# A transformer block on one core: projections moved ahead of a sum over values, gathered rows combined tile by tile, a table read one step sooner

## What is computed

```python
h = _layernorm(x) * (1 + ca) + sa
q = einsum('bpm,hmd->bphd', h, Q_w) + Q_b      # k and v likewise
logits = where(causal_mask, NEG, einsum('bqhd,bkhd->bhqk', q, k) / sqrt(128))
attn = einsum('bhqk,bkhd->bqhd', softmax(logits), v)
x = x + ga * (einsum('bqhd,hdm->bqm', attn, O_w) + O_b)
h = _layernorm(x) * (1 + cb) + sb
...
topk_scores, topk_idx = top_k(softmax(h @ Wr + router_bias), 4)
yb = einsum('ech,ehd->ecd', silu(xb @ Wg) * (xb @ Wu), Wd)     # xb: the tokens of each expert's slots
out[tok] += yb[eid, pos] * w                                    # 4 rows of yb per token
out = out + einsum('nsh,shd->nd', silu(h @ Sg) * (h @ Su), Sd)  # shared part
x = x + gb * out
```

## Time and profile before

| | us |
|---|---|
| median of 3 runs | 2115.46 |
| lowest and highest run | 2114.06, 2116.05 |
| the profiled execution, its time | 2119.06 |
| the profiled execution, its span | 2117.3 |

### The profile page before, as it was taken

The page is one execution under the profiler, slowest core; times in us unless marked ns, Lnnn a source line. Parts: engine busy times, 40 slices in busy tenths (PEclk is TensorE's granted clock), DMA queues, the critical chain, the costliest instruction groups (busy, mean ns, idle before and its releaser), DMA issues.

```text
span 2117.3 us, 33076 instructions
## 1 busy us (share of the span) xinstructions
PE 2014.0 (95%) x9863; PEld 1501.2 (71%) x9865; DVE 1381.3 (65%) x3219; ACT 1103.8 (52%) x1638; POOL 386.7 (18%) x409
## 2 busy tenths in 40 slices
PE   6899999999999999999999999999999989999997
PEld 4667667676676677676676776667877768777775
DVE  7677686686686686776866866846545833333375
ACT  3566575676575575665766755623333134444310
POOL 5211010010110110110100101633000132222364
PEclk8999999999999999999999999999999999999998
DMA  6488888888888878878888888994431098989664
GB/s 214 95 162 161 162 162 162 162 162 161 159 165 162 173 151 171 166 156 165 162 162 161 162 161 164 214 212 151 129 106 30 1 299 286 312 279 324 187 191 152
DMA packets 932173, 366.06 MB, mean 173 GB/s; under 512 B 754800, under 2 KB 885920, under 8 KB 932128
## 3 DMA queue, kind: packets, MB, share of 16 engines
q1 hardware_dynamic: 921888, 331.93, 69.5%
q0 software_dynamic: 10240, 33.56, 5.2%
HBM read 138.86 MB, written 41.94 MB: 85 GB/s over the span
## 4 chain that ended last, share of the span: by engine, by line
PE 65%; SPq 15%; DMA 8%; DVE 4%; issue 4%; POOL 3%; ACT 1%; DVEq 0%; POOLq 0%; ACTq 0%
SPq L473 14%; PE gen L1559 9%; PE gen L1561 9%; PE gen L1560 9%; PE strip L1559 7%; PE strip L1560 6%; PE strip L1561 6%; PE strip L1851 4%; PE pv L1559 4%; PE pv L1561 3%; PE pv L1560 3%; DMA wd_sb<-in_L_ffn_Wd 3%; DMA pT<-p_lo 2%; PE strip L1858 2%; DVE acc L1541 1%
## 5 line engine op out<-in xcount | busy, mean ns | idle before, releaser
L1171 DVE SCALAR_TENSOR_TENSOR p_lo<-exps,rinv,p_hi 128x512 f16<-128x512 f32 (+3 forms) x256 | 395.4, 1560 | 27.9 <-ACT p_hi L864 24.3
L855 ACT ACTIVATE exps<-exps,nbias 128x128 f32<-128x128 f32 (+15 forms) x256 | 306.3, 1197 | 136.7 <-DVE nbias L1157 136.7
L864 ACT ACTIVATE p_hi<-exps,rinv 128x512 f16<-128x512 f32 (+3 forms) x256 | 338.1, 1351 | 15.1 <-DVE rinv L1166 6.7
L1559 PE MATMUL strip<-kT_hi,qT_hi 128*128 128x512 f32 (+3 forms) x640 | 238.3, 372 | 14.4 <-DVEq L1248 6.3
L1147 DVE TENSOR_SCALAR_CACHE_REDUCE exps<-strip 128x512 f32<-128x512 f32 x384 | 249.1, 685 | 1.8 <-PE strip L1561 1.8
L1559 PE MATMUL pv<-pT,v 128*128 128x512 f16 (+3 forms) x640 | 223.3, 349 | 21.0 <-DMA pT<-p_lo 19.7
L1560 PE MATMUL strip<-kT_lo,qT_hi 128*128 128x512 f32 (+3 forms) x640 | 234.4, 366 | 0.0
L1561 PE MATMUL strip<-kT_hi,qT_lo 128*128 128x512 f32 (+3 forms) x640 | 234.1, 366 | 0.0
L710 POOL TENSOR_TENSOR wq_lo<-wq_raw,wq_hi 128x512 fp32r<-128x512 f32 x16 | 20.8, 1300 | 1105.2 <-ACT wq_hi L834 1105.2
L1560 PE MATMUL pv<-pT,v 128*128 128x512 f16 (+3 forms) x640 | 222.1, 347 | 0.0
L1561 PE MATMUL pv<-pT,v 128*128 128x512 f16 (+3 forms) x640 | 218.8, 347 | 0.0
(11 more groups left out here) (237 smaller groups left out, 4433.5 us busy)
## 6 DMA issues: line engine op xcount, KB each, us to landing
at_dram<-at_f SPq DMA_DIRECT2D x64, 256.0 KB, 2.6
wg_sb<-in_L_ffn_Wg SPq DMA_DIRECT2D x64, 256.0 KB
wu_sb<-in_L_ffn_Wu SPq DMA_DIRECT2D x64, 256.0 KB
wd_sb<-in_L_ffn_Wd SPq DMA_DIRECT2D x64, 256.0 KB
yb_dram<-yb SPq DMA_DIRECT2D x64, 256.0 KB
a_f<-at_dram SPq DMA_DIRECT2D x58, 256.0 KB, 2.9
pT<-p_hi SPq DMA_TRANSPOSE x320, 3.3
pT<-p_lo SPq DMA_TRANSPOSE x320, 3.3
```

The source lines that it names most:

```text
L855: nc.scalar.activation(row, row, ACT.Exp, bias=nbias[:, t:t + 1], accum_out=rsum[:, t:t + 1]).then_inc(row_probs, 1)
L864: nc.scalar.activation(p_hi16[:, 0:j + 1, t, :], row, ACT.Copy, scale=rinv[:, t:t + 1]).then_inc(p_hi, 1)
L1171: nc.vector.scalar_tensor_tensor(p_lo16[:, 0:j + 1, t, :], row, rinv[:, t:t + 1], p_hi16[:, 0:j + 1, t, :], ALU.mult, ALU.subtract).then_i ...
L1559: nc.tensor.matmul(o, a_hi, b_hi, start=start, stop=False)
```

## The change

Three edits. In stage 0 of every head, PE projects the next block's queries and keys ahead of the sum over values (values stay behind it); ACT and DVE take those two projections out before they make the probabilities of the block. In the last stage each of the 16 tiles is combined by itself, one or two per step from step 1 to 10, instead of in pairs with their operations interleaved. And the table of slots is read in step 10 instead of step 11.

The tables:

```diff
-        COMBINE = {step: pair for pair, step in enumerate((2, 3, 4, 6, 7, 8, 9, 10))}
+        COMBINE = {1: (0, 1), 2: (2, 3), 3: (4,), 4: (5, 6), 5: (7, 8), 6: (9,), 7: (10, 11), 8: (12, 13), 9: (14,),
+                   10: (15,)}
...
-                   11: [("table", 1)]}
+                   10: [("table", 1)]}
```

ACT, `stage`:

```diff
-                probs_hi(h, j, prev, 0)
-                probs_hi(h, j, prev, 1)
-                exp_row(h, j, 2)
-                exp_row(h, j, 3)
-                probs_hi(h, j, prev, 2)
-                probs_hi(h, j, prev, 3)
+                if j == 0:
+                    exp_row(h, j, 2)
+                    exp_row(h, j, 3)
+                    gen_hi_of("q", nxt[1], nxt[0])
+                    gen_hi_of("k", nxt[1], nxt[0])
+                    for t in range(TB):
+                        probs_hi(h, j, prev, t)
+                else:
...
                 if j == 0:
                     take_at_scale(h)
-                if nxt is not None:
+                    gen_hi_of("v", nxt[1], nxt[0])
+                elif nxt is not None:
                     for kind in "qkv":
                         gen_hi_of(kind, nxt[1], nxt[0])
```

DVE, `stage`:

```diff
+                if j == 0:
+                    row_inverse(h, j, 2)
+                    row_inverse(h, j, 3)
+                    gen_out_of("q", nxt[1], nxt[0])
+                    gen_out_of("k", nxt[1], nxt[0])
+                    probs_lo(h, j, 0)
+                    probs_lo(h, j, 1)
+                else:
...
```

DVE, `combine_beside`:

```diff
-                for k in range(TOPK):
-                    for t in pair:
-                        if k == 0:
-                            dve.wait_ge(g_landed[t % GATHS], (t // GATHS + 1) * 16 * TOPK)
-                        else:
-                            dve.wait_ge(dve_step, steps[0] - 1)
...
-                dve.sem_inc(combined, 2)
-                dve.sem_inc(gath_free, 2)
+                for t in COMBINE[step]:
+                    dve.wait_ge(g_landed[t % GATHS], (t // GATHS + 1) * 16 * TOPK)
+                    for k in range(TOPK):
+                        link(nc.vector.scalar_tensor_tensor(acc[:, t, :], gath[t % GATHS][:, k, :], w_top[:, t, k:k + 1],
+                                                            acc[:, t, :], ALU.mult, ALU.add))
+                    dve.sem_inc(combined, 1)
+                    dve.sem_inc(gath_free, 1)
```

PE, `stage`:

```diff
                 score(h, j)
+                if j == 0:
+                    project("q", *reversed(nxt))
+                    project("k", *reversed(nxt))
                 if prev is not None:
...
                     sum_values(hp, jp)
                 if nxt is not None:
                     hn, jn = nxt
-                    project("q", jn, hn)
-                    project("k", jn, hn)
+                    if j > 0:
+                        project("q", jn, hn)
+                        project("k", jn, hn)
```

More of the change, by code:

```diff
@@ L890, in stage @@
                 exp_row(h, j, 1)
-                probs_hi(h, j, prev, 0)
-                probs_hi(h, j, prev, 1)
-                exp_row(h, j, 2)
-                exp_row(h, j, 3)
-                probs_hi(h, j, prev, 2)
-                probs_hi(h, j, prev, 3)
+                if j == 0:
[6 more added lines that the diff above has]
+                else:
+                    probs_hi(h, j, prev, 0)
+                    probs_hi(h, j, prev, 1)
+                    exp_row(h, j, 2)
+                    exp_row(h, j, 3)
+                    probs_hi(h, j, prev, 2)
+                    probs_hi(h, j, prev, 3)
                 if prev is not None:
@@ L1180, in stage @@
                 score_row(h, j, 3)
-                probs_lo(h, j, 0)
-                row_inverse(h, j, 2)
-                probs_lo(h, j, 1)
-                row_inverse(h, j, 3)
+                if j == 0:
[6 more added lines that the diff above has]
+                else:
+                    probs_lo(h, j, 0)
+                    row_inverse(h, j, 2)
+                    probs_lo(h, j, 1)
+                    row_inverse(h, j, 3)
                 probs_lo(h, j, 2)
@@ L1188, in stage @@
                     hn, jn = nxt
-                    gen_out_of("q", jn, hn)
-                    gen_out_of("k", jn, hn)
+                    if j > 0:
+                        gen_out_of("q", jn, hn)
+                        gen_out_of("k", jn, hn)
                     if jn == 0:
@@ L1532, in combine_beside @@
                     return
-                pair = (2 * COMBINE[step], 2 * COMBINE[step] + 1)
                 dve.wait_ge(down_out, OUT_AFTER + step // (SC - AFTER0) * TB)
-                for k in range(TOPK):
-                    for t in pair:
-                        if k == 0:
-                            dve.wait_ge(g_landed[t % GATHS], (t // GATHS + 1) * 16 * TOPK)
-                        else:
-                            dve.wait_ge(dve_step, steps[0] - 1)
-                        ins = nc.vector.scalar_tensor_tensor(acc[:, t, :], gath[t % GATHS][:, k, :],
-                                                             w_top[:, t, k:k + 1], acc[:, t, :], ALU.mult, ALU.add)
-                        steps[0] += 1
-                        ins.then_inc(dve_step, 1)
-                dve.wait_ge(dve_step, steps[0])
-                dve.sem_inc(combined, 2)
-                dve.sem_inc(gath_free, 2)
+                for t in COMBINE[step]:
[5 more added lines that the diff above has]
+                    dve.sem_inc(gath_free, 1)
             for c in (6, 7):
```

## The result

The changed kernel took 2178.52 us (median of 4 runs, 2175.89 to 2180.56), the kernel before 2114.76 beside it (2113.86 to 2116.05): ratio 1.030, interval 1.0282 to 1.0318, so 3% slower. The forecast was 2180. The profiled execution took 2175.89 us with a span of 2174.1; the one of before had a span of 2117.3.

The account below looks back on a forecast made before the run. PE, busy 95% of the span, was taken as the bound. Heads +43.5, first head +6.3, clock +28, table -6.5 and combining -7 gave +64.3 us on 2119.06, 2183.4, stated as 2180 against the median; range 2146 to 2203.

Parts of the forecast that it names:

- The wait in each head: Later 15 heads: ACT waits for the values' transpose to land, PE ends 2.9 us later per head, +43.5 us.
- The first head: First head: probabilities made only after the keys' copy, so the values' transpose goes out later, +6.3 us.
- The clock: Behind PE's new idle stretch in 16 heads, matmuls run at half clock, 1.75 us each: +28 us, bounds 0 and 48.
- The rival in which the clock holds: Heads: everything as forecast but without the 28 us for the clock, 2152 us; chance 15%.
- Faster, with the values in time: Heads: the values' transpose lands in time, each head gains 1.9 us, 2073 us in all; chance 9%.
- The table: Start of the experts: slot table read a step earlier, PE's wait and the low clock behind it go, -6.5 us.
- The combining: Last stage: POOL's two waits go (5.1 us) and fewer operations follow the last gather (1.8 us), -7 us.
- The lower bound: Combining: +2 us if DVE, waiting in a step for a late tile, holds up PE's down product as often as now.
- The sum: Whole kernel: +43.5 + 6.3 + 28 - 6.5 - 7 = +64.3 us, forecast 2180 us at 60%.
- its rival: Heads: the low clock lasts as long as the 5.9 us stretch, 1.25 us more in 16 heads, 2200 us; chance 12%.

Follow-up runs that it names:

- e4: Changed kernel with a buffer of its own for block 0's values in heads 1 to 15: 2085.71 us, ratio 0.9859 to the kernel before.
- e5: Changed kernel with SP issuing the transpose of block 0's values two transposes earlier, no new buffer: 2117.89 us, ratio 1.0001 to the kernel before.
- e7: Changed kernel with 18 matmuls that nobody reads filling PE's stand in each head: 2153.43 us, ratio 1.0182 to the kernel before.
- e8: e4 with the first head's query and key copies back in the order of before: 2079.70 us, ratio 0.9834 to the kernel before.
- e3: Kernel before with only the combining tile by tile: 2115.31 us, ratio 1.0003 to the kernel before.
- e1: Kernel before with only the new order in the heads, old table and combining: 2186.48 us, ratio 1.0332 to the kernel before.
- e2: Kernel before with only the slot table read in step 10: 2109.25 us, ratio 0.9975 to the kernel before.
- e10: e3 with five tiles combined one step later: 2110.48 us, ratio 0.9975 to the kernel before.
- e12: e8 with the tiles' combining spread over steps 1 to 11 by when they land: 2069.22 us, ratio 0.9785 to the kernel before.
- e6: Changed kernel with ACT's and DVE's order of before in all heads, PE's order new: 2172.37 us, ratio 1.0268 to the kernel before.

## Why the prediction was right, point by point

**The wait in each head** was in the prediction as a chain of two conditions: SP's first transpose is held to the third group's end, and ACT's write to `vT` is held to the landing of a transpose behind it. Both hold. e4 cuts the second and e5 shortens the queue between the two, and either takes the wait's loss away. PE's stand was forecast at 5.3 us and came to 4.6, ACT's wait at 4.5 and came to 6.1, and a head's end was forecast 2.9 us later and measured at 2.5: the values' issue came 13.81 us after the sum's start where 13.98 was reckoned (741.23 - 727.25), and the landing took 3.08 instead of 3.16. The rest is a gap of 0.15 us that stood between the scores and the sum before and is gone with the new order.

**The first head** was +6.5 us, forecast 6.3. Its values' transpose was issued at 86.08, forecast 86.7; the scores of this trace start 0.5 us sooner, so the two agree to 0.1.

**The clock** was the largest unknown, 28 us between bounds of 0 and 48. In the profiled executions a head costs 1.9 us by it, forecast 1.75, and e7 gives back 25 us in all. The rival in which the clock holds (2152) is what e7 measured with the clock held: 2153. That is closer than it should be, since e7 has the terms in it that missed. The kernel before spent none of the stretch from 180 to 1300 us at the low level, the change 60 us, part of it while PE stood. In the Trainium skill, "TensorE: Matmul & The Clock Gate", Part 1, the ramp penalty is put at under 1% of a typical kernel span; the sentence stands beside the slow matmuls of a kernel's start. Here the filled stands gave back 25 us of 2178, 1.2% (0.8 to 1.5), for a loss that comes again in every head. The 21 us that the prediction took from that figure, an estimate, lie within the interval, so the run does not decide between them and the 28 of the rows.

**Faster, with the values in time** (2073, 9%), did not happen in the change, and its mechanism is the one that e4 builds: 80.2 us a head, forecast 80.3. The price of 2073 left out the first head's 6.3 us, which don't hang on the later heads, and had the combining's 7 in it; e4 measured 2085.7, and with the first head mended (e8) 2079.7.

**The table** was forecast at -6.5 and measured at -5.3 (2.5 to 8.0) by itself.

**The combining** is the step that failed. It was forecast at -7 and measured at +0.6 (-1.3 to +2.5) by itself in e3, and at about -1.5 by what e1 and e2 leave of the whole (1.0300 - 1.0332 + 0.0025). The prediction put it as "POOL's own pace then sets the end, so I don't credit PE's waits for hs_lo beyond this", and added up POOL's two waits and the shorter tail behind the last gather. Both effects came. But the price was taken behind the last tile, and the end no longer hangs on that one. The chain leaves the gathers with tile 13, 96.3 us into the stage, and from there to the end it is 31.0 us, with PE's 5.34 for hs_lo in them; before it was the last tile at 112.2 and 15.9 us. So POOL's pace does set the end, but what was saved behind the last tile was off the path, and PE's waits for hs_lo, which the prediction left aside, were on it (16.6 us before, 15.3 in the change, 18.2 in e3). e10 and e12, which change only the steps in which tiles are combined, shorten these waits and the stage. The lower bound, +2 "if DVE, standing in a step for a late tile, holds up PE's down product as often as now", describes what happened; I gave it too little weight, although the row with 4.29 us of DVE waiting for a gather was in view.

**The sum.** +70 for the heads against 77.8 forecast (of the 7.8 us too many, some 6 are the 0.4 us too many in each head's wait), -5 for the table against -6.5, about nothing for the combining against -7: two errors of about 7 us with opposite signs. 2180 was met to 1.5 us, which is closer than the terms deserve; that much of it is luck.

## What to carry to other kernels

When an engine's work is moved ahead of a step that frees a buffer, follow the buffer's chain over the other queues to the next engine that needs it. Here 1.9 us gained on TensorE became 2.5 us lost, by one shared buffer and two issues on SP's queue. A swap of the issues undoes the loss, and a second buffer turns it into a gain. A new stand of a few microseconds on TensorE should be priced with the clock behind it. And a wait for a transfer on an engine that others feed on should stand in the step where the transfer has landed: moving five tiles by one step was worth half as much as leaving out three quarters of the work on all sixteen.

## What the runs showed of the hardware that I had not expected

The same stand of 4.6 us was followed by low stretches of two lengths. In the change ten of the low stretches behind the steady heads' stands last 3.4 us and five last 6.8, the first 0.8 to 1.3 us of these still within the stand. The head behind a long one takes 87.2 to 87.45 us, the others 86.0 to 86.4. Behind the resumption at 352.12 the low level lasts until 355.9, behind that at 264.67 until 270.6. The windows of the change behind 264.67:

```profile
268.00:269.00 1.00, 1.00 (x4) 0.81 (x3) 0.86 (x6) 0.76 (x2) 0.00 (x0) 0.50 1.05 313
269.00:270.00 1.00, 1.00 (x3) 0.30 (x3) 0.30 (x2) 1.00 (x2) 0.00 (x0) 0.50 0.82 237
270.00:271.00 1.00, 1.00 (x5) 0.45 (x4) 0.93 (x4) 0.78 (x3) 0.00 (x0) 0.72 0.18 53
```

The two lengths are near the 3.7 and 5.9 us from which the prediction drew its price and its rival. Here both occur within one execution, so the truth lay between them; what decides between them no run here shows.

A stand of 2.0 to 2.1 us kept the clock in 13 of e5's 15 steady heads. Behind the resumptions at 584.47, after 2.10 us, and at 1324.98, after 2.07 us, it fell for 3.4 us, and the first of these heads took 83.7 us instead of 82.1:

```profile
586.00:587.00 1.00, 1.00 (x4) 0.80 (x3) 0.96 (x6) 0.95 (x3) 0.00 (x0) 0.50 0.45 85
```

Stands of 3.7 to 3.9 us in e6 lost it in all 15 steady heads, for 3.4 us in ten of them and 6.8 in five. So a stand of some 2 us is not safe or unsafe by its length alone; what decided in those two heads is open.

Four dependent additions of one tile on VectorE took 3.11 us, 0.78 each, while the interleaved order of before needed 4.73 for seven, 0.68 each. The change gives up 0.1 us an operation for freeing a tile earlier, some 6 us of VectorE's time over the 64; the total of e3 does not show them.
